# A sixteen-entry decoder on one core: the order of the last three entries, and half of the first entry's mixing products on VectorE

## The chip, the cores and the metric

One Trainium2 chip, one of its cores. The metric is the device time of one execution of the whole program in microseconds (us), less is better. TensorE is called PE in the views, VectorE DVE, ScalarE ACT, GpSimd POOL, and SP is the engine that issues all DMA transfers here.

## What is computed

Sixteen independent batch entries of 256 tokens by 256 features run through six layers, each followed by a layer norm. Cut to what matters:

```python
x = _layernorm(x + _L0_attn_ref(x, ...))      # q, k, v per token; kv and qkv mix the 16 heads of ONE token; then a gelu MLP
x = _layernorm(x + _L0_xattn_ref(x, ctx, ...))  # 16 heads, window of 64 to either side
x = _layernorm(x + _L0_ffn_ref(x, ...))       # a cell of 6 nodes, each an 8-head attention
x = _layernorm(x + _L1_attn_ref(x, ...))      # causal, linear, 16 heads
x = _layernorm(x + _L1_xattn_ref(x, ctx, mask, ...))  # 16 heads against the context
x = _layernorm(x + _L1_ffn_ref(x, ...))       # a product with a matrix made from a Fourier transform
```

In the first layer each token has its own small product over heads:

```python
kv = jnp.einsum('bhnd,bhne->bnde', k, v)
qkv = jnp.einsum('bhnd,bnde->bhne', q, kv)
```

The kernel computes it as q k for each pair of heads of a token, and then that times v. This is what is called mixing below.

## The kernel before

Four entries are in flight at a time (`NS = 4`), each in its own slots of SBUF. Entry i + 4 is loaded when entry i is finished. The work of an entry is a list of steps, made by `entry_steps`: each names its engine, an operation, a cost in us that is only a planning number, what it needs and which PSUM banks it takes and frees. `setup_steps` does the same for the work that is done once: products of weights (`fold`, `cb`, `four`, `nb`, `ob`, `n5`), for which TensorE multiplies and VectorE or ScalarE evicts, and `scale`, six pairs of scalings of weights on GpSimd (L1627, L1628).

`program_plan` plays these steps through with the planning costs and writes down, engine by engine, the order in which they came. That order is what every engine then executes: an engine never passes over a step that waits. Among the steps that are ready on an engine the planner takes the one of the lowest entry number first (the set-up counts as 1.5, on SP as 2.5), and among those the one with the longest chain of steps behind it (`tail`). The tails are multiplied by random factors drawn from the numbers in `SEEDS`, so that a different list of seeds gives a different order among steps of one entry. A tail is the same for all entries. The planner also chooses the PSUM banks (`pick`): a score product takes two pairs of banks, most others one.

The steps that the text speaks of:

- `mix1` and `mix2`: the mixing of an entry, in 16 pieces of two heads. For each piece GpSimd makes the products q k (L1641) and VectorE sums them (L1217), then GpSimd multiplies by v (L1651) and VectorE sums again (L1221). Pieces of one parity share a buffer. `mixn` divides (L1226, L1228, L1232), then `o_t` transposes the result on TensorE (L733), and the entry goes on with `a_o`, `fc`, `down`.
- Attention heads come as `s` (scores, L886), `nm` (the negated row maxima transposed, L896), `st` (scores transposed and the maxima added, L908 and L920), `pv` (L947), for the nodes of the cell also L954. VectorE takes the maxima (L1260) and splits them (L1266, L1269), ScalarE takes the exponentials (L1491). An entry has 4 groups in the second layer, 12 in the cell, and 4 in the fifth layer, the groups 16 to 19, called the y heads.
- `r_t` to `rpv`: the fourth layer. `y_t`, `y_q`, `y_o`, `f_t`, `f`: the last two. All products of a whole weight matrix are L740 or L748.
- `store` writes the entry's result (L1770).

The middle of the program is periodic: from one entry to the next TensorE gets the same 146 steps.

## Time and profile before

| | |
|---|---|
| median of 3 runs | 3439.23 us (3435.72 to 3452.06) |
| the profiled execution | 3441.86 us, its span 3440.1 us |
| PE busy | 3101.7 us, 90% of the span |
| DVE, ACT, POOL busy | 2330.8, 1701.0, 1182.5 us |
| mean granted clock of TensorE | 0.967 of full speed |

The span is from the first instruction of the program to the last; the time is 1.8 us longer. A busy TensorE is one with a matmul on it, at whichever clock. The granted clock is full (1.0, 2.4 GHz) or half (0.5, 1.2 GHz), and a number between these says how a stretch was shared.

### The profile page before, as it was taken

Reading aid. Unit: us, or ns where it says so; the run is one execution under the profiler, and the core shown is the slowest. Engines: PE = TensorE matmul, PEld = TensorE weight load, DVE = VectorE, ACT = ScalarE, POOL = GpSimd, SP = SyncE. Lnnn points to the kernel's source line nnn. Section 1 sums busy time; section 2 is a strip of 40 time slices with the busy share of each in tenths; the row PEclk is TensorE's granted clock in tenths of the full one; section 3 lists DMA queues with packets and bytes.
Section 4 is the critical chain, followed back from the end, with each engine's and each line's share of the span. In section 5 each row is a group of like instructions: output and inputs, shape, how many; then the busy total and the mean of one; then the engine's idle time right before and its main releaser. Section 6 shows DMA issues by size and latency. Waiting matters only on the chain.

```text
span 3440.1 us, 75934 instructions
## 1 busy us (share of the span) xinstructions
PE 3101.7 (90%) x29836; PEld 2294.8 (67%) x29836; DVE 2330.8 (68%) x5044; ACT 1701.0 (49%) x3496; POOL 1182.5 (34%) x1308
## 2 busy tenths in 40 slices
PE   7889889999999999989999999999999999989876
PEld 6766666676666666666666766666676666666654
DVE  6586667768686866768677686867767686465543
ACT  1245454555546455554545555464554545454442
POOL 7876007062341615234170623416052341100000
PEclk8899999999999999999999999999999999999996
DMA  7211001010101101011110101011010110100000
GB/s 223 72 56 35 20 29 35 26 47 20 43 27 38 29 26 47 20 39 32 35 32 25 49 20 43 27 38 29 22 52 20 39 32 20 32 14 10 10 10 4
DMA packets 123275, 122.77 MB, mean 36 GB/s; under 512 B 9776, under 2 KB 122672, under 8 KB 122800
## 3 DMA queue, kind: packets, MB, share of 16 engines
q1 hardware_dynamic: 122928, 117.91, 11.6%
q8 instruction: 246, 4.03, 0.5%
q14 instruction: 101, 0.83, 0.1%
HBM read 113.69 MB, written 4.19 MB: 34 GB/s over the span
## 4 chain that ended last, share of the span: by engine, by line
PE 63%; DVE 15%; ACT 7%; POOL 7%; issue 7%; DMA 1%; SPq 0%; DVEq 0%; POOLq 0%; ACTq 0%
PE banks L748 18%; PE banks L740 16%; PE banks L886 7%; DVE nmx L1260 6%; PE banks L947 5%; PE banks L908 5%; ACT work L1491 4%; POOL work L1641 3%; PE banks L733 2%; POOL work L1651 2%; PE banks L954 2%; PE banks L851 2%; POOL work L1661 1%; DVE added L1278 1%; ACT work L1393 1%
## 5 line engine op out<-in xcount | busy, mean ns | idle before, releaser
L748 PE MATMUL banks<-work,weights 128*128 128x256 f32 x3584 | 848.6, 385 | 22.5 <-DVE work L1284 10.4
L748 PEld LDWEIGHTS banks<-work,weights 128*128 128x128 f32 x3584 | 662.5, 190 | 153.6 <-issue 43.4
L1260 DVE TENSOR_REDUCE nmx<-banks 128x4 f32<-128x1024 f32 (+1 forms) x567 | 609.5, 1115 | 200.5 <-PE banks L886 199.0
L1491 ACT ACTIVATE work<-banks 128x1024 f32<-128x1024 f32 (+3 forms) x703 | 598.4, 908 | 270.5 <-PE banks L920 251.4
L740 PE MATMUL banks<-weights,work 128*128 128x256 f32 x2688 | 665.8, 395 | 20.2 <-DVE work L1288 7.6
L740 PEld LDWEIGHTS banks<-weights,work 128*128 128x128 f32 x2688 | 506.6, 195 | 131.9 <-issue 37.0
L1651 POOL TENSOR_TENSOR work<-work 128x512 f32<-128x512 f32 x256 | 417.6, 1655 | 85.1 <-DVE work L1221 81.9
L908 PE MATMUL banks<-work 32*128 32x256 f32 (+1 forms) x5120 | 367.1, 397 | 70.1 <-DVE nmx L1260 42.1
L886 PE MATMUL banks<-work 32*128 32x256 f32 (+1 forms) x5120 | 361.2, 398 | 70.5 <-DVE nmx L1260 29.7
L1641 POOL TENSOR_TENSOR work<-work 128x512 f32<-128x512 f32 x256 | 335.5, 1333 | 132.0 <-DVE work L1217 108.6
L1695 POOL TENSOR_TENSOR work<-work,row 128x512 f32<-128x512 f32 x64 | 93.0, 1463 | 836.8 <-PE banks L733 836.8
L1278 DVE TENSOR_TENSOR added<-work 128x1024 f32<-128x1024 f32 x192 | 264.4, 1378 | 150.3 <-ACT work L1491 111.1
L908 PEld LDWEIGHTS banks<-work 32*128 32x128 f32 x5120 | 235.8, 189 | 191.2 <-DVE nmx L1260 81.0
L947 PE MATMUL banks<-work 128*32 128x256 f32 (+3 forms) x5632 | 333.6, 358 | 31.3 <-DVE nmx L1260 15.6
L886 PEld LDWEIGHTS banks<-work 32*128 32x128 f32 x5120 | 238.9, 189 | 158.4 <-issue 102.3
L947 PEld LDWEIGHTS banks<-work 128*32 128x32 f32 x5632 | 157.0, 109 | 172.9 <-issue 96.5
L1393 ACT ACTIVATE work<-banks,cb 128x256 f32<-128x256 f32 x384 | 160.8, 470 | 202.8 <-PE banks L748 202.8
L1217 DVE TENSOR_REDUCE work<-work 128x32 f32<-128x512 f32 x256 | 172.5, 683 | 127.0 <-POOL work L1641 127.0
L1661 POOL TENSOR_SCALAR_AFFINE_SELECT work<-work 128x128 f32<-128x128 f32 (+1 forms) x512 | 161.2, 362 | 256.2 <-ACT work L1491 256.2
L1221 DVE TENSOR_REDUCE work<-work 128x32 f32<-128x512 f32 x256 | 173.0, 681 | 87.1 <-POOL work L1651 86.9
L1475 ACT ACTIVATE work<-banks 128x256 bf16<-128x256 f32 x320 | 116.7, 387 | 162.4 <-PE banks L896 162.2
L1254 DVE CUSTOM_DVE_ANT_0 banks<-banks,band 128x192 f32<-128x192 f32 x512 | 165.7, 393 | 27.5 <-PE banks L886 27.4
(160 smaller groups left out, 3540.7 us busy)
## 6 DMA issues: line engine op xcount, KB each, us to landing
weights<-in_w_all SPq DMA_DIRECT2D x322, 256.0 KB, 2.7
work<-in_w_setup SPq DMA_DIRECT2D x41, 256.0 KB, 5.0
work<-in_ctx SPq DMA_DIRECT2D x32, 256.0 KB, 3.0
work<-in_x SPq DMA_DIRECT2D x16, 256.0 KB, 3.0
out<-work SPq DMA_DIRECT2D x16, 256.0 KB, 2.2
weights<-in_w_all SPq DMA_DIRECT2D x1, 3072.0 KB, 15.6
row<-in_rows SPq DMA_DIRECT2D x1, 1280.0 KB, 9.0
mrow<-in_mask SPq DMA_DIRECT2D x16, 32.0 KB, 3.3
```

The source lines that it names most:

```text
L740: ins = e.matmul(b[:, m * 256:m * 256 + 256], xin[:, k, m * P:m * P + P], wslot(w)[:, k, :], start=(k == 0 and (m == 0 or closed)) if star ...
L748: ins = e.matmul(b[:, m * 256:m * 256 + 256], wslot(w)[:, k, m * P:m * P + P], xin[:, k, :], start=(k == 0 and (m == 0 or closed)) if star ...
L886: ins = e.matmul(b[g // 2][g % 2][:, cc * 256:cc * 256 + kk.stop - kk.start], q[32 * g:32 * g + 32, f, cc * P:cc * P + P], k[32 * g:32 * g ...
L908: e.matmul(b[g // 2][g % 2][:, o], k[32 * g:32 * g + 32, f, kc * P:kc * P + P], q[32 * g:32 * g + 32, f, qq], start=(kc == 0), stop=False, ...
L947: ins = e.matmul(b[32 * g:32 * g + 32, lo:hi], left, right[:, kc * 256 + lo - qq.start:kc * 256 + hi - qq.start], start=(kc == 0), stop=(k ...
L1260: ins = e.tensor_reduce(nmax(s, n)[:, 2 * p + j:2 * p + end, :], b.rearrange("p j (c n) -> p j c n", c=NC)[:, :, :, 0:w], AX, ALU.max, neg ...
L1278: e.tensor_tensor(added[:, half], pt(half, 0, 4)[:, :, 0:S], pt(half, 0, 4)[:, :, S:2 * S], ALU.add).then_inc(*tell(vec[s], "added", a, i))
L1393: ins = e.activation(dst[:, c, :], halves(src)[:, c, :], ACT.Identity, scale=w(c) if w else 1.0, bias=bias(c) if bias else 0.0)
L1491: ins = e.activation(dst, b.rearrange("p j (c n) -> p j c n", c=NC)[:, :, :, 0:w], ACT.Exp)
L1641: e.tensor_tensor(big1, q.unsqueeze(2).broadcast_to([P, PH, NH, DH]), k.unsqueeze(1).broadcast_to([P, PH, NH, DH]), ALU.mult).then_inc(*te ...
L1651: e.tensor_tensor(big2, mix.unsqueeze(2).broadcast_to([P, PH, DH, NH]), v.unsqueeze(1).broadcast_to([P, PH, DH, NH]), ALU.mult).then_inc(* ...
L1661: ins = e.affine_select(out=part, in_=part, compare_op=ALU.is_ge, fill=0.0, base=base, pattern=[[0, 2], [sign, hi - lo]], channel_multipli ...
```

## The change

Two rules of the planner change, and the list of seeds.

1. In the choice among ready steps the entry's number is replaced by `min(w[0], NB - 3)`. For entries 0 to 12 nothing changes; 13, 14 and 15 are equal, and among them the step with the longest chain behind it goes first.
2. For entry 0 the odd pieces' `mix1` and `mix2` products are put on VectorE. They become the operations `product1` and `product2`, with a planning cost of 0.65 us. These are 16 products, with the same operands as GpSimd's.
3. `SEEDS` loses one number in the middle and gets four new ones at the end.

```diff
-SEEDS = (519167, ..., 279811, 642892, 207843, ..., 237616)
+SEEDS = (519167, ..., 279811, 207843, ..., 237616, 902168, 809533, 586745, 617725)
...
+    def engine(i, n):
+
+        e, op, a = steps[n][:3]
+        return "DVE" if i == 0 and e == "POOL" and op in ("mix1", "mix2") and a % 2 else e
+
...
-                waiting[steps[n][0]].append((i, -tail[n], n))
+                waiting[engine(i, n)].append((i, -tail[n], n))
...
-                    ((2.5 if e == "SP" else 1.5) if w[0] < 0 else w[0]) + (0 if kept_mode(w[2]) else 0.5), w[1], w[2])):
+                    ((2.5 if e == "SP" else 1.5) if w[0] < 0 else min(w[0], NB - 3)) + (0 if kept_mode(w[2]) else 0.5), w[1], w[2])):
...
+                if steps[n][0] == "POOL" and e == "DVE":
+                    op, us = {"mix1": "product1", "mix2": "product2"}[op], 0.65
...
+                elif op == "product1":
+                    q, k, v, mix, big1, big2 = mix_views(s, a)
+                    if a < 2:
+                        e.wait_ge(*when("elu", 0, i))
+                        e.wait_ge(*when("elu", 1, i))
+                    else:
+                        e.wait_ge(*when("mix", a - 2, i))
+                    e.tensor_tensor(big1, q.unsqueeze(2).broadcast_to([P, PH, NH, DH]),
+                                    k.unsqueeze(1).broadcast_to([P, PH, NH, DH]), ALU.mult).then_inc(
+                        *tell(vec[s], "mix products", a, i))
+                elif op == "product2":
+                    q, k, v, mix, big1, big2 = mix_views(s, a)
+                    e.wait_ge(*when("mix", a, i))
+                    if a < 2:
+                        e.wait_ge(*when("a_qkv", 2, i))
+                    else:
+                        e.wait_ge(*when("mix sum", a - 2, i))
+                    e.tensor_tensor(big2, mix.unsqueeze(2).broadcast_to([P, PH, DH, NH]),
+                                    v.unsqueeze(1).broadcast_to([P, PH, DH, NH]), ALU.mult).then_inc(
+                        *tell(vec[s], "mix values", a, i))
```

The new lines shift the line numbers: what is L733, L740, L748, L886, L896, L908, L920, L947 before is L740, L747, L755, L893, L903, L915, L927, L954 in the changed kernel, and the VectorE lines L1207, L1212, L1217, L1221 are L1214, L1219, L1224, L1228. The new products are L1236 and L1246.

TensorE, the end of the program. Before, the last rows are the y heads of entry 15 and its `y_o`, `f_t`, `f`:

```order
L908 MATMUL banks<-work 128x256 x8
L920 MATMUL banks<-work,ones_bf 128x512 x4
L896 MATMUL banks<-ident_bf,nmx 128x128 x4
L947 MATMUL banks<-work 32x256 x8
L908 MATMUL banks<-work 128x256 x8
L920 MATMUL banks<-work,ones_bf 128x512 x4
L947 MATMUL banks<-work 32x256 x8
L908 MATMUL banks<-work 128x256 x8
L920 MATMUL banks<-work,ones_bf 128x512 x4
L947 MATMUL banks<-work 32x256 x16
L740 MATMUL banks<-weights,work 128x256 x4
L733 MATMUL banks<-ident,work 128x128 x4
```

In the changed kernel the same place holds the last `st` and `pv` of entries 14, 15 and 13, then `f` of 13, `y_o` of 14 and 15 in one row of 12, and `f_t` and `f` of 14 and of 15:

```order
L954 MATMUL banks<-work 32x256 x8
L915 MATMUL banks<-work 128x256 x8
L927 MATMUL banks<-work,ones_bf 128x512 x4
L954 MATMUL banks<-work 32x256 x8
L740 MATMUL banks<-ident,work 128x128 x4
L954 MATMUL banks<-work 32x256 x8
L747 MATMUL banks<-weights,work 128x256 x12
L740 MATMUL banks<-ident,work 128x128 x4
L747 MATMUL banks<-weights,work 128x256 x4
L740 MATMUL banks<-ident,work 128x128 x4
L747 MATMUL banks<-weights,work 128x256 x4
```

Three entries' ends now stand among each other. In the planner's lists, TensorE's last 62 of 2366 steps are entry 15's alone before; in the changed kernel entry 13 has its last step 7 from the end, and the last 104 steps hold all of `r_t` to `f` of the entries 13, 14 and 15. Entry 12 ends 335 steps (4326 matmul records) before the end in the one, 326 steps (4158 records) in the other.

VectorE, the first mixing. Before, after the bias additions (L1207) and the second half of the elu (L1212), there are only sums of the mixing (L1217, L1221) and evictions of set-up products (L1129, L1125):

```order
L1212 SCALAR_TENSOR_TENSOR work<-work 128x512 x2
L1207 TENSOR_TENSOR work<-banks,row 128x512
L1212 SCALAR_TENSOR_TENSOR work<-work 128x512
L1207 TENSOR_TENSOR work<-banks,row 128x512
L1217 TENSOR_REDUCE work<-work 128x32 x2
L1221 TENSOR_REDUCE work<-work 128x32
L1129 TENSOR_TENSOR cb<-banks,ews 128x3x2
L1221 TENSOR_REDUCE work<-work 128x32
L1217 TENSOR_REDUCE work<-work 128x32
L1207 TENSOR_TENSOR work<-banks,row 128x512
L1217 TENSOR_REDUCE work<-work 128x32
L1125 TENSOR_SCALAR weights<-banks,ews 128x512
```

In the changed kernel at the same place:

```order
L1219 SCALAR_TENSOR_TENSOR work<-work 128x512 x2
L1214 TENSOR_TENSOR work<-banks,row 128x512
L1236 TENSOR_TENSOR work<-work 128x512
L1219 SCALAR_TENSOR_TENSOR work<-work 128x512
L1224 TENSOR_REDUCE work<-work 128x32 x2
L1246 TENSOR_TENSOR work<-work 128x512
L1236 TENSOR_TENSOR work<-work 128x512
L1228 TENSOR_REDUCE work<-work 128x32
L1224 TENSOR_REDUCE work<-work 128x32
L1228 TENSOR_REDUCE work<-work 128x32
L1246 TENSOR_TENSOR work<-work 128x512
L1224 TENSOR_REDUCE work<-work 128x32
```

All 16 products (L1236, L1246) and nearly all sums of entry 0 stand ahead of the first eviction of a set-up product, which before was the seventh of these rows. On GpSimd three of the six scalings now stand between the even pieces' products of entry 0; before, the first came after them all.

TensorE, the y heads of one entry in the periodic middle. Before, two `st` (L908, L920) follow four `s`:

```order
L886 MATMUL banks<-work 128x256 x8
L896 MATMUL banks<-ident_bf,nmx 128x128 x2
L886 MATMUL banks<-work 128x256 x8
L908 MATMUL banks<-work 128x256 x8
L920 MATMUL banks<-work,ones_bf 128x512 x4
L908 MATMUL banks<-work 128x256 x8
L920 MATMUL banks<-work,ones_bf 128x512 x4
L896 MATMUL banks<-ident_bf,nmx 128x128 x4
L947 MATMUL banks<-work 32x256 x8
```

and in the changed kernel the first `st` comes after two `s`, and `s`, `pv` and `st` alternate:

```order
L893 MATMUL banks<-work 128x256 x8
L903 MATMUL banks<-ident_bf,nmx 128x128 x4
L755 MATMUL banks<-work,weights 128x256 x4
L915 MATMUL banks<-work 128x256 x8
L927 MATMUL banks<-work,ones_bf 128x512 x4
L893 MATMUL banks<-work 128x256 x8
L903 MATMUL banks<-ident_bf,nmx 128x128 x2
L954 MATMUL banks<-work 32x256 x8
L893 MATMUL banks<-work 128x256 x8
L915 MATMUL banks<-work 128x256 x8
L927 MATMUL banks<-work,ones_bf 128x512 x4
```

In the periodic middle some 20 of 146 TensorE steps stand in another order, all of them here, and one pair of cell products (`ck` and `eq`) changes places twice.

## Rows read from the trace of the kernel before

**Rows 1.** The page: span, and PE busy and granted clock in 40 slices

```profile
span 3440.1 us, 75934 instructions
...
PE   7889889999999999989999999999999999989876
...
PEclk8899999999999999999999999999999999999996
```

**Rows 2.** SP's timeline: the stores of entries 12 and 15 (start, duration)

```profile
2909.84 0.38 SPq L1770 DMA_DIRECT2D out<-work  x1
...
3437.52 0.38 SPq L1770 DMA_DIRECT2D out<-work  x1
```

**Rows 3.** Stretch, its us, busy PE, PEld, DVE, ACT, POOL (instructions), PEclk, DMA

```profile
2909.80:3106.00 196.20, 179.60 (x1850) 131.60 (x1846) 110.21 (x254) 103.89 (x212) 20.42 (x50) 0.98 0.07 22
3106.00:3296.00 190.00, 169.60 (x1689) 120.57 (x1689) 103.94 (x194) 93.02 (x189) 10.73 (x23) 0.95 0.04 11
3296.00:3440.00 144.00, 91.16 (x764) 63.86 (x762) 56.50 (x108) 44.26 (x92) 4.51 (x6) 0.77 0.02 6
```

**Rows 4.** The same for two periods of the middle

```profile
903.40:1101.70 198.30, 183.57 (x1840) 135.31 (x1841) 144.30 (x312) 105.88 (x219) 73.57 (x79) 1.00 0.11 33
...
1908.10:2107.50 199.40, 183.96 (x1841) 135.38 (x1840) 144.15 (x311) 106.09 (x219) 72.93 (x79) 1.00 0.12 33
```

**Rows 5.** PE by line and shape, 3296 to 3440: busy, mean ns, idle

```profile
L740 PE MATMUL banks<-weights,work 128*128 128x256 f32 x80 | 24.4, 462 | 7.9 <-DVE work L1288 2.8 <-ACT work L1418 2.3 <-DVE work L1284 1.5
L908 PE MATMUL banks<-work 32*128 32x256 f32 x128 | 13.6, 558 | 3.7 <-ACT work L1475 2.1 <-issue 1.4 <-ACT work L1491 0.2
```

**Rows 6.** The same for the period 1707 to 1908

```profile
L740 PE MATMUL banks<-weights,work 128*128 128x256 f32 x168 | 40.4, 386 | 0.3 <-DVE work L1284 0.2
...
L908 PE MATMUL banks<-work 32*128 32x256 f32 x256 | 18.2, 398 | 4.2 <-DVE nmx L1260 3.5 <-issue 0.7
```

**Rows 7.** PE's longest waits, 3296 to 3440: total, times, longest

```profile
PE banks L733 <- DVE work L1201: 12.5, 3, 6.7
PE banks L896 <- DVE nmx L1269: 10.4, 3, 4.1
```

**Rows 8.** Busy time by stretch: `r_t` to the end, and `y_o` to the end

```profile
3355.00:3440.00 85.00, 52.50 (x436) 36.79 (x436) 32.36 (x67) 24.76 (x53) 3.52 (x4) 0.70 0.01 4
3422.90:3440.00 17.10, 7.50 (x20) 4.92 (x20) 4.85 (x14) 1.59 (x5) 1.26 (x1) 0.63 0.05 15
```

**Rows 9.** GpSimd and VectorE by line during the first mixing, 27.8 to 86.6

```profile
L1651 POOL TENSOR_TENSOR work<-work 128x512 f32<-128x512 f32 x18 | 27.4, 1536 | 2.0 <-DVE work L1217 2.0
L1641 POOL TENSOR_TENSOR work<-work 128x512 f32<-128x512 f32 x18 | 23.5, 1318 | 2.2 <-DVE work L1217 2.2
...
L1217 DVE TENSOR_REDUCE work<-work 128x32 f32<-128x512 f32 x18 | 12.0, 680 | 3.7 <-POOL work L1641 3.7
```

**Rows 10.** Timelines of VectorE and GpSimd, 85 to 92

```profile
85.97 0.69 DVE L1232 TENSOR_TENSOR work<-work,head 128x512 f32<-128x512 f32 x1
...
86.74 1.27 POOL L1667 TENSOR_TENSOR work<-work,row 128x512 f32<-128x512 f32 x1 [3.01 <-DVE work L1232]
...
90.43 1.58 POOL L1627 TENSOR_SCALAR weights<-weights,ewb 128x512 f32<-128x512 f32 x1
```

**Rows 11.** Two VectorE lines in the whole run: duration ns min/median/max, first and last start

```profile
L1212 DVE SCALAR_TENSOR_TENSOR work<-work x32: 682/691/1929, 25.1 to 2729.5; 128x512 f32<-128x512 f32 x32
...
L1159 DVE TENSOR_TENSOR weights<-weights,wsum x2: 1695/1696/1697, 52.1 to 62.2; 128x512 f32<-128x512 f32 x2
```

**Rows 12.** PE's timeline: entry 0's `o_t`

```profile
86.87 0.60 PE L733 MATMUL banks<-ident,work 128*128 128x128 f32 x4
```

**Rows 13.** Busy time by stretch: the start, in two parts

```profile
14.10:86.90 72.80, 66.21 (x285) 57.42 (x286) 50.68 (x91) 9.00 (x18) 56.63 (x41) 0.79 0.69 220
86.90:152.10 65.20, 55.32 (x293) 46.63 (x291) 39.61 (x92) 16.24 (x33) 61.52 (x46) 0.94 0.31 90
```

**Rows 14.** Busy time by stretch: y heads of entry 7, from the third `s`

```profile
1862.50:1884.60 22.10, 17.16 (x254) 10.32 (x253) 14.13 (x31) 13.95 (x24) 0.00 (x0) 1.00 0.01 2
```

More of the change, by code:

```diff
@@ L71 @@
 RSLOT = {n: i for i, n in enumerate(ROWS)}
[L73 removed]
+SEEDS = (519167, 634534, 875864, 704644, 851259, 37516, 529412, 612800, 351972, 744357, 284174, 279811, 207843, 86077, 805968, 561942, 32633, 126238, 798516, 91813, 237616, 902168, 809533, 586745, 617725)
 SLOTS = 10
```

1 line of the change is left out of this document (removed).

## Prediction, made before the changed kernel ran

> **What bounds the kernel now.** I read the page first: TensorE is the busiest engine, and the 40 slices show it at eight or nine tenths everywhere but in the last three, where the granted clock falls in the last one too [rows 1]. Then the stretches between stores. In the periodic middle one entry costs 198.3 us, of which TensorE is busy 183.6, and the next sample reads 184.0 of 199.4; so the pace of the middle is 92.4% busy at a clock of 1.00 [rows 4]. VectorE has 144 us of work in the same time and GpSimd 73. The middle is bound by TensorE, and there only fewer gaps can help.
>
> The end is another thing. Entry 12's store is issued at 2909.8 and entry 15's at 3437.5 [rows 2], those of 13 and 14 at 3106 and 3296, and in the three stretches from store to store TensorE is busy 179.6 of 196.2 us, 169.6 of 190.0, and 91.2 of 144.0 us [rows 3]. In the last stretch entry 15 is alone. The reader is to see two losses in it: 53 us without a matmul, and a granted clock of 0.77, at which the same matmul takes longer: L740 462 ns in place of 386, L908 558 in place of 398 [rows 5, 6]. The idle time is that of one chain of steps with nothing beside it: TensorE waits for a layer norm's last step on VectorE (12.5 us in 3 waits) and for the split maxima (10.4 us) [rows 7].
>
> **The end, costed.** First the size of the pool. The two dearest lines of the last stretch would cost 24.4 x 386/462 = 20.4 and 13.6 x 398/558 = 9.7 us at full clock, 7.9 us less than they do [rows 5, 6]; I take 4.3 us more for the other 53 us of matmuls, so 79 of the 91.2 us remain. After entry 12's store there are then 179.6 + 169.6 + 79 = 428 us of TensorE work. At the pace of the middle (92.4%) that is 463 us; it takes 530.2 us now. So 67 us is the most that a perfect end gives back. By stretch: 2 us in the first, 6 in the second, 59 in the last. Three entries in flight are thus as good as four, two nearly, one is not.
>
> The change keeps three entries in flight until the last hundred steps, so nearly all of the lone stretch is gone. What is paid for it: the three entries reach the same layer together. From `r_t` to the end, entry 15 alone takes 85.0 us, with 32.4 us of VectorE and 52.5 us of TensorE at a clock of 0.70 [rows 8]. At full clock I estimate TensorE at 43 us of it: the last 144 us lose 12 of 91 us to the clock, 13%, and with 0.30 in place of 0.23 missing from the clock that becomes 18% of 52.5. Three times this is 129 us of TensorE and 97 us of VectorE. At the middle's pace it would be 140 us. VectorE has 0.75 of TensorE's work here and 0.78 in the middle [rows 4], so no engine takes TensorE's place as the bound; but the chain score, maxima, split, transposition, exponential, product is gone through by twelve groups of heads at the same time on 8 banks, with no long product of another layer to cover it. I take 20 us on top of the 140, half way between no loss (0) and 40 us. The very last steps, `y_o` to the end, are one chain in either kernel: 17.1 us with 7.5 busy [rows 8], of which two other entries can fill only the beginning; 10 us are lost. So 30 of the 67 us are paid again, and the end gains **37 us** (bounds: 67 - 10 = 57 us with no loss but the chain, and 67 - 10 - 40 = 17 us).
>
> Entry 12 itself ends 168 matmul records later; at 199 us for 1840 records [rows 4] its store comes 18 us later than before. This costs nothing, since the work that went ahead of it is no longer to do behind it.
>
> **The start, costed.** TensorE's first product waits 14 us for the first layer norm, which stays. Entry 0's `o_t` runs at 86.9 us [rows 12], 0.2 us after its mixing ends. In the mixing GpSimd makes 36 products in 50.9 us and waits 4.2 [rows 9]; 32 are entry 0's. GpSimd is the bound of entry 0 there. The change takes 16 products of 1.32 and 1.54 us away, 22.9 us, and puts three pairs of scalings in between that came behind (1.58 us each [rows 10], 9.5 us in all). It leaves a gain of 13.4 us if a product on VectorE costs what such an instruction costs alone, 0.69 us for 512 columns [rows 10].
>
> It does not. The instruction with that price, L1232, ran while GpSimd was idle for 3.01 us [rows 10]. L1159 is the same operation on 512 columns with both operands in SBUF, ran twice while GpSimd multiplied, and took 1.70 us both times; L1212, with two SBUF operands too, takes 691 ns in the median and up to 1929 [rows 11]. The sums, with one operand, show no such spread. So a VectorE product beside a stream of GpSimd products waits for the one under way, and the stream in turn waits for it. I price the 16 products at 1.4 us, nearer to L1159 than to the 0.69 of an idle GpSimd (bounds 0.69 and 1.93), with some 11 us of waiting on VectorE, and 16 x 0.69 = 11 us that GpSimd's stream is held up. That leaves 13.4 - 11 = 2.4 us of the gain.
>
> The Trainium skill says so in general ("SBUF — State Buffer", section "Who interferes with whom"): a VectorE instruction with two SBUF inputs and a GpSimd instruction that reads SBUF exclude each other for a whole instruction, and the later one blocks. The trace agrees, with 1.70 against 0.69 us. By a VectorE product at 0.69 us the start would gain 13 us; by this rule it gains next to nothing.
>
> What is queued behind matters as well: on VectorE nearly the whole mixing now stands ahead of the evictions of the set-up products. TensorE has only 8 banks; after nine set-up products and biases it must wait for the VectorE queue. Before, it worked through them with 6.6 us idle up to `o_t` [rows 13]. VectorE has 16 products at 1.4, 27 sums at 0.68 [rows 9] and some 3.5 us of other work from 25 us on, so it frees the bank that the fold of `v` of node 0 needs at about 69 us, where TensorE wants it at about 56 (that is when it made this product before). Some 10 us of idle come in there. They are partly paid back, since the postponed products then fill later gaps: 86.9 to 152.1 has 9.9 us idle [rows 13]. Sum for the start: -2.4 + 10 - 7, taken as **0 us** (bounds -12 and +15).
>
> **The middle, costed.** No operation is added. The y heads of each entry stand in another order: from the third `s` to the following layer TensorE is busy 17.2 of 22.1 us, 4.9 us idle [rows 14]. That is what a better order can win at most and, I assume, as much as a worse one would lose. In the new order the first exponential starts about a score product earlier, but the first `pv` then waits for it with one product in between where there were two. These nearly cancel; I take 0.4 us gained per entry, for the 13 entries that pass through it in this form: **-5 us** (bounds, at 1 us per entry to either side, -13 and +13).
>
> **Sum.** -37 + 0 - 5 = -42 us on the profiled execution's own 3441.9 us: 3399.9. That execution is 2.7 us over the median of the three runs, so against the median I predict **3397 us**, 1.2% less.
>
> **The rivals.**
> *The end keeps the middle's pace* (chance 0.14): TensorE and VectorE interlock without loss, as in the stretch 2909.8 to 3106, which has three entries in it and a clock of 0.98 [rows 3]. Against it: those three were in different layers. Then 57 us at the end, 5 in the middle: 3377 us.
> *VectorE holds up the start* (0.16): the products cost 1.9 us, the banks come free later still, and the 7 us are not paid back: +15 us. With the rest as forecast 3412 us.
> *The new order of the y heads is worse* (0.07): TensorE stands idle 3 us more per entry, in place of 0.4 less; over 13 entries 39 us, which cancels the gain: 3441 us. For it: TensorE's waits in this place are already for VectorE's maxima. Against: the operations and their number are the same.
> *The three ends do not overlap* (0.05), the case on the other side. If the twelve groups of y heads and the layer norms of the three entries form one chain through VectorE, `r_t` to the end takes three times 85.0 us = 255 us [rows 8], against the 170 us of my sum (140 + 20 + 10). That is 85 us more: 3482 us. It decides from about 212 us on, where the gain of 42 is used up. Against it: the stretch with two entries lost only 6 us.
>
> **How the numbers follow.** The forecast itself has a chance of 0.58. Its own range is 3378 to 3415 us. Less than 0.5%, 17 us, can't be told from no change here. Below 3422 lie the forecast, the first rival, and most of the second: faster 0.86. Between 3422 and 3456 lie the third and the unlucky sums of small losses: 0.09. Slower 0.05. For 8 times in 10 the range reaches from a bit under the first rival to a bit over the second: 3362 to 3428 us.
>
> **What the profile would show.** The stores of 13, 14 and 15 within about 15 us of each other at the end, and entry 12's some 18 us later than now. From entry 12's store to the end 465 to 485 us, in place of 530. The granted clock near 0.95 until some 20 us before the end. the last 104 TensorE steps in some 170 us. L1236 and L1246 with a mean near 1.4 us, and not 0.69. Entry 0's `o_t` at 80 to 87 us, with a wait of TensorE for VectorE's fold evictions ahead of it. The distance between middle stores within 1 us of 199.5. The forecast is wrong if the three last entries wait for each other's banks or VectorE by more than the 20 us that I gave them, or if the middle's period moves by more than 1 us, since that counts thirteen times.

## The result, and the profile after

The changed kernel takes 3425.77 us in the median, the kernel before 3449.28 us in the runs beside it; the ratio is 0.9941, 95% interval [0.9924, 0.9959], a gain of 20 us. The ratio and its interval leave out one execution of each kernel that took far longer (4289 and 9857 us). Forecast were 42 us and a range of 3378 to 3415 us. The direction is right and the size is not.

The profiled execution of the changed kernel takes 3425.71 us, 16 less than that of before. Its page (span; PE busy and granted clock in 40 slices):

```profile
span 3424.0 us, 75954 instructions
...
PE   6988999998998999999999999999989988999987
...
PEclk8899999999999999999999999999999989999999
```

Against [rows 1] the last three slices of PE read 987 where they were 876, and the clock does not fall at the end. In exchange there are new eights at the 33rd and 34th slice, and the clock falls in the 33rd, 2739 to 2825 us, ahead of entry 12's store. SyncE's timeline has the stores (start, duration):

```profile
2958.92 0.38 SPq L1797 DMA_DIRECT2D out<-work  x1
...
3409.35 12.36 SPq L1797 DMA_DIRECT2D out<-work  x3
```

The last three stores lie within 12.4 us of each other, but entry 12's comes 49 us later than in [rows 2]. The profiled change is then +49 up to that store and -65 behind it, in all -16. Busy time by stretch (stretch; us; busy PE, PEld, DVE, ACT, POOL; clock; DMA share; GB/s):

```profile
2733.90:2952.80 218.90, 187.42 (x1899) 137.85 (x1895) 151.86 (x411) 105.17 (x219) 92.84 (x137) 0.91 0.10 29
2952.80:3424.00 471.20, 421.90 (x4170) 298.25 (x4166) 266.34 (x477) 233.10 (x470) 13.83 (x19) 0.95 0.03 10
2958.90:3424.00 465.10, 416.65 (x4112) 294.74 (x4104) 260.45 (x465) 231.63 (x465) 13.51 (x18) 0.95 0.03 10
3280.80:3424.00 143.20, 116.86 (x1341) 82.77 (x1340) 104.74 (x231) 75.74 (x170) 11.53 (x14) 0.95 0.07 22
```

From entry 12's store to the end it takes 465 us instead of 530, at a clock of 0.95; the last row is the last 104 steps. That part of the forecast held. The first row does not fit it: 146 steps, a period's number, take 219 us, and TensorE is idle for 31 of them. In the middle a period has 15 us of idle time [rows 4].

For all later comparisons I place the steps of TensorE's order in the trace by counting matmul records. Step 1747 is the last mark at which the kernels are still in the middle, at step 1893 entry 12 is at its third node, step 2039 is where entry 12 has just ended.

| us | start to step 1747 | 1747 to 1893 | 1893 to 2039 | 2039 to end of TensorE |
|---|---|---|---|---|
| before | 2511.8 | 201.5 | 204.4 | 516.7 |
| changed | 2519.9 | 214.0 | 218.9 | 465.4 |

The end gives 51 us. The 292 steps ahead of it take 27 us more, and the start and middle 8. The 8 are no cost of the edits: ten of the runs below have, with the changed kernel's order of TensorE from step 287 to step 1747, 2003 to 2036 us in it, where the changed kernel has 2014 and before 2006. The 12 to 15 us of the stretch 1747 to 1893 are more than such a spread: the orders without the early levelling take 198.5 to 204.3 us there, and the changed kernel and the two runs with its order there (E6, E18) 214.0 to 215.1.

### The profile page after: what moved, and what is told of

Same layout as the page of the kernel before. It is cut to its first block, busy times and chain, and to the rows that moved or that the text cites. A ratio compares the mean times of both kernels' runs of the same rounds, so it can differ in the third digit from the quotient of the medians.

```text
span 3424.0 us, 75954 instructions
## 1 busy us (share of the span) xinstructions
PE 3101.5 (91%) x29836; PEld 2290.3 (67%) x29836; DVE 2353.5 (69%) x5040; ACT 1701.8 (50%) x3495; POOL 1167.6 (34%) x1292
## 4 chain that ended last, share of the span: by engine, by line
PE 61%; DVE 14%; POOL 10%; issue 7%; ACT 7%; DMA 1%; SPq 0%; DVEq 0%; POOLq 0%; ACTq 0%
PE banks L755 18%; PE banks L747 14%; PE banks L893 7%; PE banks L954 6%; PE banks L915 6%; DVE nmx L1287 5%; POOL work L1668 5%; ACT work L1518 3%; POOL work L1688 3%; PE banks L740 2%; POOL work L1678 2%; PE banks L858 2%; PE banks L961 2%; PE banks L927 1%; DVE added L1305 1%
## 5 line engine op out<-in xcount | busy, mean ns | idle before, releaser
L755 PE MATMUL banks<-work,weights 128*128 128x256 f32 x3584 | 857.8, 388 | 15.1 <-ACT work L1518 6.5
L755 PEld LDWEIGHTS banks<-work,weights 128*128 128x128 f32 x3584 | 668.4, 192 | 151.0 <-issue 48.7
L747 PE MATMUL banks<-weights,work 128*128 128x256 f32 x2688 | 658.6, 392 | 14.7 <-DVE work L1311 5.2
L747 PEld LDWEIGHTS banks<-weights,work 128*128 128x128 f32 x2688 | 501.3, 193 | 124.8 <-issue 41.0
L893 PE MATMUL banks<-work 32*128 32x256 f32 (+1 forms) x5120 | 363.5, 399 | 83.6 <-DVE nmx L1287 31.7
L1678 POOL TENSOR_TENSOR work<-work 128x512 f32<-128x512 f32 x248 | 406.9, 1663 | 85.1 <-DVE work L1228 83.2
L915 PE MATMUL banks<-work 32*128 32x256 f32 (+1 forms) x5120 | 371.3, 400 | 60.6 <-DVE nmx L1287 36.4
L1668 POOL TENSOR_TENSOR work<-work 128x512 f32<-128x512 f32 x248 | 330.3, 1354 | 133.4 <-DVE work L1224 110.3
L954 PE MATMUL banks<-work 128*32 128x256 f32 (+3 forms) x5632 | 336.8, 361 | 34.5 <-POOL work L1688 24.8
L915 PEld LDWEIGHTS banks<-work 32*128 32x128 f32 x5120 | 237.9, 190 | 175.2 <-issue 101.4
L893 PEld LDWEIGHTS banks<-work 32*128 32x128 f32 x5120 | 240.0, 189 | 171.4 <-issue 114.8
L954 PEld LDWEIGHTS banks<-work 128*32 128x32 f32 x5632 | 158.3, 110 | 178.4 <-issue 120.7
L1224 DVE TENSOR_REDUCE work<-work 128x32 f32<-128x512 f32 x256 | 171.8, 682 | 107.1 <-POOL work L1668 107.0
L1688 POOL TENSOR_SCALAR_AFFINE_SELECT work<-work 128x128 f32<-128x128 f32 (+1 forms) x512 | 161.6, 362 | 241.0 <-ACT work L1518 241.0
L1228 DVE TENSOR_REDUCE work<-work 128x32 f32<-128x512 f32 x256 | 172.8, 680 | 83.2 <-POOL work L1678 83.0
L1281 DVE CUSTOM_DVE_ANT_0 banks<-banks,band 128x192 f32<-128x192 f32 x512 | 165.4, 391 | 34.7 <-PE banks L893 34.4
```

Of the source, the lines that this page charges most:

```text
L747: ins = e.matmul(b[:, m * 256:m * 256 + 256], xin[:, k, m * P:m * P + P], wslot(w)[:, k, :], start=(k == 0 and (m == 0 or closed)) if star ...
L755: ins = e.matmul(b[:, m * 256:m * 256 + 256], wslot(w)[:, k, m * P:m * P + P], xin[:, k, :], start=(k == 0 and (m == 0 or closed)) if star ...
L893: ins = e.matmul(b[g // 2][g % 2][:, cc * 256:cc * 256 + kk.stop - kk.start], q[32 * g:32 * g + 32, f, cc * P:cc * P + P], k[32 * g:32 * g ...
L915: e.matmul(b[g // 2][g % 2][:, o], k[32 * g:32 * g + 32, f, kc * P:kc * P + P], q[32 * g:32 * g + 32, f, qq], start=(kc == 0), stop=False, ...
L954: ins = e.matmul(b[32 * g:32 * g + 32, lo:hi], left, right[:, kc * 256 + lo - qq.start:kc * 256 + hi - qq.start], start=(kc == 0), stop=(k ...
L1228: e.tensor_reduce(q, big2, AX, ALU.add).then_inc(*tell(vec[s], "mix sum", a, i))
```

## Experiments

All ratios are to the kernel before, timed beside it on the same chip. The lines of a kernel with the late rule (E7, E9, E10, E11, E15, E16) are one higher than those of the changed kernel.

### Which of the three edits is it? (E1 to E4)

The edits are: the numbers (`SEEDS`), the products (`engine`), the rule (`min(w[0], NB - 3)`). Each kernel is the changed one with some of them undone:

```diff
 E1  -SEEDS = (... of the change)   +SEEDS = (... of before)
 E1  -        return "DVE" if i == 0 and ... else e   +        return e
 E2  -SEEDS = (... of the change)   +SEEDS = (... of before)
 E2  -... min(w[0], NB - 3)   +... w[0]
 E3  -        return "DVE" if i == 0 and ... else e   +        return e
 E3  -... min(w[0], NB - 3)   +... w[0]
 E4  -... min(w[0], NB - 3)   +... w[0]
```

E1, the rule only. 

> Only the rule for the last three entries, with the numbers and the mixing of before. Theory A (the rule itself pushes entry 12 back: with entries 13 to 15 equal, the work of 14 and 15 that fills entry 12's gaps is other work than before, and the x layer's selects queue behind their mixing on GpSimd): entry 12's store comes 25 to 45 us later than in before (2935 to 2955 us), the stretch after it is some 65 us shorter, and the whole is 15 to 25 us faster. Theory B (the new numbers cost the time, the rule gives the full gain that was forecast): entry 12's store comes some 5 us from before's and the whole is 35 to 50 us faster. Theory C (the products on VectorE cost it): as B.

E2, the products only. 

> Only the first entry's odd products on VectorE, with the numbers and the priorities of before. Theory A: within 5 us of before. Theory B: within 5 us. Theory C: 10 to 25 us slower, with the first entry's o_t steps later than 86.9 us or the middle's periods longer than 199 us.

E3, the numbers only. 

> Only the new list of numbers. Theory A: within 5 us of before, periods of the middle within 1 us of 199. Theory B: 10 to 25 us slower, of it some 8 us in the middle (that much later step 1747 of TensorE's order) and the rest after it. Theory C: within 5 us of before.

E4, numbers and products without the rule. 

> The changed kernel without the rule for the last three entries (new numbers, and products on VectorE). Theory A: within 5 us of before, with entry 12's store at 2905 to 2920 us. Theory B and C: 15 to 30 us slower than before, since the loss is there and the gain of the end is not; entry 12's store at 2930 to 2945 us.

| | ratio | 95% interval |
|---|---|---|
| E1 rule only | 0.9998 | 0.9976 to 1.0021 |
| E2 products only | 1.0478 | 1.0452 to 1.0505 |
| E3 numbers only | 1.0394 | 1.0366 to 1.0421 |
| E4 numbers and products | 0.9996 | 0.9976 to 1.0017 |

E4 says that numbers and products together are worth nothing (1 us, within 8), so on the new numbers the gain is the rule's: 0.9941 / 0.9996 = 0.9945, 19 us, known to some 9 us. In E1 the rule gains nothing at all on the old numbers: from step 1747 to 2039 it takes 451 us (before 406), from there 463 (before 517). Theory A thus named the right two stretches, and the loss ahead is still larger than it had said; entry 12's store comes at 2962.6 us, later than its 2935 to 2955. No theory had expected the figures of E2 and E3. Neither edit touches an instruction of the middle, and yet every period of the middle (steps 287 to 1747) takes 202 to 228 us in place of 198 to 205. The changes are not additive: each edit alone costs 135 to 165 us, of which 124 to 127 in the middle, and both together cost nothing.

### Do the products cost that, or the order? (E5, E6)

E5 takes the plan of before as it is and moves the 16 products from one engine's list to the other's after planning; E6 moves them back in the plan of the changed kernel.

```diff
+    taken = [(t, (i, names[op], a, u)) for t, (i, op, a, u) in timed["POOL"] if i == 0 and op in names and a % 2]
+    plan["POOL"] = [s for _, s in timed["POOL"] if not (s[0] == 0 and s[1] in names and s[2] % 2)]
+    plan["DVE"] = [s for _, s in sorted(timed["DVE"] + taken, key=lambda v: v[0])]
```

E5. 

> The kernel before, with the order of every engine as it was, but the first entry's 16 odd products taken out of GpSimd's order and put into VectorE's at the places of their planned times. E2 moved them and let the planner lay out everything anew, and took 165 us more. Theory A (it is the order that the planner makes from the changed starting times, above all in the middle, that cost the 165 us): within 12 us of before. Theory B (the products themselves hold up VectorE and, through it, the rest): 100 us and more slower.

E6. 

> The changed kernel with its order on every engine, but the 16 products put back on GpSimd at the places of their planned times. Theory A (the move is worth nothing by itself, as its o_t came 4.6 us earlier and step 287 at the same time): within 5 us of the changed kernel, that is a ratio to before of 0.989 to 0.998. Theory B (GpSimd's longer chain, 11 us more by the durations of rows 9 and 11, decides the start): 8 to 12 us slower than the changed kernel, ratio 0.996 to 1.000.

E5: 1.0022 [0.9997, 1.0047], E6: 0.9950 [0.9928, 0.9972] (the changed kernel had 0.9941 in its own comparison). E5 thus costs 8 us (-1 to +16) and not 165: the 165 us of E2 are the order that the planner laid out anew around the products. Theory A held there. E6 does not decide between its theories. Its ratio is 3 us from the changed kernel's, but the interval reaches into theory B's 0.996 to 1.000, and its one profiled execution, the slowest of its twelve, shows theory B's size at the start: `o_t` at 93.6 us and step 287 at 518.5, against 82.3 and 505.9 with the products on VectorE. The nine other runs with the changed kernel's start reach step 287 at 500.8 to 506.6. So within the new order the products on VectorE give some 12 us up to there by that one profile, and what is left of it at the end isn't known.

### Does the order cost because it never repeats? (E13, E14)

In before and in the changed kernel the planned order of a period's 146 steps takes only three forms over the middle, in E2 it is another one in every period, in E3 one comes back only after four. Adding one number to the old list gives orders of either kind:

```diff
 E13 -..., 237616)   +..., 237616, 3)
 E14 -..., 237616)   +..., 237616, 6)
```

E13. 

> The kernel before with one number (3) added at the end of its list. Its planned order of TensorE's steps differs from entry to entry up to step 1163 and from there to step 2039 is the same 146 steps for each entry. Theory A (an order that does not repeat costs, whatever edit made it): periods of 207 to 220 us up to step 1163 and of 198 to 206 us behind it; ratio 1.010 to 1.030. Theory B (the harm of E2 and E3 lies in their own edits): within 10 us of before.

E14. 

> The kernel before with one number (6) added at the end of its list; its planned order is another one for each of the twelve periods. Theory A: periods of 207 to 222 us all along, ratio 1.035 to 1.055 as in E2 and E3. Theory B: within 10 us of before.

E13: 1.0465 [1.0436, 1.0493]. E14: 1.0455 [1.0427, 1.0483]. Two periods of E13 in its repeating half:

```profile
2000.20:2218.70 218.50, 194.32 (x1844) 140.73 (x1840) 142.70 (x313) 105.96 (x220) 72.02 (x79) 0.95 0.10 29
2218.70:2433.80 215.10, 191.44 (x1845) 139.25 (x1841) 142.91 (x313) 105.80 (x220) 71.91 (x79) 0.96 0.11 32
```

My theory fell on its own prediction: E13's repeating periods take 214 to 220 us, longer than several of its irregular ones (205 to 209). What both runs do show is that one more random number, and nothing else, makes this kernel 4.6% slower. E14's ratio lies where theory A had it, but after E13 this doesn't speak for the theory. The work is the same: 143 us of VectorE, 106 of ScalarE and 72 of GpSimd, as in [rows 4]. TensorE is idle 24 us per period instead of 15, and its clock is 0.95 to 0.96 instead of 1.00, and the same 1840 or so matmuls take 8 to 11 us longer. Which property of an order does it stays open. TensorE's waits in E13 (line waited at, engine and line waited for; us, times, longest), 1226 to 2400 us:

```profile
PE banks L908 <- DVE nmx L1260: 16.4, 18, 1.4
PE banks L886 <- DVE nmx L1260: 12.9, 12, 1.7
PE banks L886 <- ACT work L1393: 10.6, 8, 1.9
PE banks L896 <- DVE nmx L1260: 8.5, 15, 0.7
```

They are many short ones for the row maxima, none of them a new kind.

### Does it matter when the entries are made level? (E7, E9 to E11, E15, E16)

```diff
+        late = any(j == NB - 4 and o == "rpv" for j, o, _, _ in plan["PE"])
         for e in waiting:
...
-... min(w[0], NB - 3)
+... (min(w[0], NB - 3) if late else w[0])
```

That is E7; it takes effect from the first of entry 12's two `rpv` steps on, TensorE's step 1975. E10 has `"f"` for `"rpv"`, E11 `"co"` of node 2. E9 and E15 are E7 and E10 with the numbers and the mixing of before. E16 is E10 with four entries (`NB - 4`, and `NB - 5` in `late`).

E7. 

> The changed kernel, with the last three entries put level only once entry 12's last step of the attention to the kept rows has been issued on TensorE. Theory A (while entry 12 runs, the levelled entries 14 and 15 fill its gaps with work that collides, 29 us of time ahead of step 2039 against E4; the drain's gain needs only the levelling behind it): entry 12's store at 2915 to 2930 us, the stretch behind it 475 to 495 us, whole 3395 to 3415 us, ratio 0.984 to 0.990. Theory B (the loss is what the drain's gain is bought with: the work of 14 and 15 done early is what is missing late): the stretch behind entry 12's store is 495 us or more and the whole within 8 us of the changed kernel.

E10. 

> As E7, but level only once entry 12's last product (the step f, TensorE's step 2030) is issued, some 52 steps later than in E7. Theory A (only work ahead of entry 12's store that the levelling pulls forward costs anything): steps 1747 to 2039 take 403 to 408 us, as without the rule, entry 12's store comes at 2915 to 2930 us, and the drain behind it still ends the three entries together, 480 to 495 us behind it; ratio within 0.003 of E7's. Theory B (what a levelling costs ahead it must pay back behind, one for one): the stretch behind entry 12's store is longer by what is saved ahead of it, and the same ratio as E7 comes out too, but with entry 12's store more than 10 us earlier and the drain more than 10 us longer.

E11. 

> As E7, but level already from entry 12's third node on (TensorE's step 1888), some 90 steps earlier than in E7 and 140 later than the changed kernel's levelling begins to show. Theory A (cost grows with how long entry 12 shares TensorE with levelled entries): entry 12's store 10 to 25 us later than in E7, ratio between E7's 0.984 and the changed kernel's 0.994. Theory B (only the first levelled steps, 1747 to 1893, cost something): within 0.002 of E7's ratio.

E9. 

> The kernel before (its numbers, its mixing) with the rule of E7, level once entry 12's attention to the kept rows is issued. Theory A (the late levelling is worth about 50 us by itself; numbers and products only decide which repeated order the middle falls into, and both repeated orders take the same time): ratio 0.981 to 0.989, with periods of the middle of 198 to 206 us. Theory B (the new list of numbers and the products are needed for the gain): ratio 0.992 to 1.000.

E15. 

> The kernel before (its numbers, its mixing) with the rule of E10: the last three entries level once entry 12's last product is issued. If the gain is the drain's alone: steps 1747 to 2039 take 403 to 410 us, step 2039 to the end 455 to 465 us instead of 517, ratio 0.982 to 0.988. If the numbers and the products have a part in it: ratio 0.989 to 0.996.

E16. 

> The changed kernel, with the last four entries level once entry 11's last product is issued. If a drain is better the more entries end together: step 1893 to the end is 10 us and more shorter than E10's. If the levelled entries wait for one another at the same kinds of step (the loss ahead in the changed kernel): steps 1893 to 2185 take 20 to 40 us more than E10's, and what the end gains over E10 is under 15 us; ratio 0.988 to 0.996.

| | level from | ratio | 95% interval | 1747 to 2039, us | idle in it | 2039 to end, us |
|---|---|---|---|---|---|---|
| changed | start | 0.9941 | 0.9924 to 0.9959 | 432.9 | 48.8 | 465.4 |
| E11 | step 1888 | 0.9869 | 0.9836 to 0.9903 | 425.8 | 46.3 | 462.2 |
| E7 | step 1975 | 0.9838 | 0.9800 to 0.9876 | 416.3 | 39.6 | 462.6 |
| E10 | step 2030 | 0.9848 | 0.9815 to 0.9880 | 404.0 | 29.1 | 457.0 |
| E4 | never | 0.9996 | 0.9976 to 1.0017 | 403.5 | 31.2 | 524.1 |
| E9 | as E7 | 0.9890 | 0.9862 to 0.9919 | 414.7 | 41.0 | 462.7 |
| E15 | as E10 | 0.9828 | 0.9800 to 0.9856 | 410.9 | 30.9 | 449.9 |
| E16 | step 1884, four entries | 0.9935 | 0.9910 to 0.9959 | 451.8 | 66.1 | 446.4 |

The columns of us are of one profiled execution each, and executions of one order differ: before, E5 and E15, whose TensorE order is the same up to step 2030, take 406, 409 and 411 us from 1747 to 2039. The sooner the levelling begins, the more is lost ahead of step 2039. By the intervals of their ratios E7, E10 and E11 are clear of the changed kernel; E11 and E7 are not told apart, and with entry 12's store at 2985.7 us, 55 after E7's, E11 missed theory A's 10 to 25. The drain behind it takes 457 to 465 us in the first four whenever it begins: what is done ahead buys nothing behind (against theory B of E7 and E10). The stretches 1893 to 2039 and 2039 to the end of E10:

```profile
2737.50:2943.00 205.50, 191.17 (x1848) 142.05 (x1849) 141.75 (x303) 109.46 (x224) 73.76 (x79) 0.99 0.12 35
2943.00:3405.70 462.70, 406.24 (x4213) 293.32 (x4211) 267.60 (x556) 232.12 (x477) 33.33 (x71) 0.96 0.04 13
```

Between E7 and E10 the profiles differ by 18 us behind step 1747 and the ratios by nothing that can be told. E15 has the lowest ratio, though its interval overlaps those of E7 and E10: the kernel before with nothing but the levelling of its last three entries from entry 12's last product on, 3393.54 against 3453.55 us, 1.7% less. New numbers and products were not needed. Its stretches were expected at 403 to 410 and 455 to 465 us; the second was shorter. E9's 0.9890 stands at the edge of what theory A gave it. E7's and E10's stores came at 2931.0 and 2930.2 us, and E10's drain takes 476 us from there, a little less than expected. E16 loses 40 us against E10 from step 1893 to 2185 and wins 15 back: four level entries lose more ahead than they win at the end.

### Which queue makes the loss ahead? (E8, E12)

```diff
 E8  +... min(w[0], NB - 3) if e != "POOL" else w[0]
 E12 +... min(w[0], NB - 3) if e == "PE" else w[0]
```

E8. 

> The changed kernel with the rule on all engines but GpSimd, where the entries keep their order. Theory A (the x layer's selects behind the mixing of entries 14 and 15 on GpSimd are the loss ahead of step 2039): TensorE's waits of line 954 on GpSimd halve there, step 2039 starts 10 to 20 us earlier than at 2952.8 us, whole 8 to 20 us faster than the changed kernel. Theory B (VectorE's row maxima and the order on TensorE are the loss): within 5 us of the changed kernel.

E12. 

> The changed kernel with its rule on TensorE's queue alone; VectorE, ScalarE and GpSimd keep the entries' order. Theory A (the loss ahead of step 2039 is made on TensorE's own order: steps of entries 14 and 15 stand between entry 12's and 13's): steps 1747 to 2039 still take 425 to 440 us, ratio 0.990 to 0.997. Theory B (it is made on VectorE and ScalarE, where maxima and exponentials of the levelled entries stand ahead of those that TensorE needs next): steps 1747 to 2039 take 403 to 415 us, ratio 0.984 to 0.990.

E8: 0.9921 [0.9897, 0.9946]; steps 1747 to 2039 take 448 us, step 2039 starts at 2952.4 us, and TensorE's waits at L954 for GpSimd's L1688 there are 5.1 us in 5, in place of 6.1 in 6. Theory A failed on all of these. E12: 0.9938 [0.9915, 0.9960], 443 us, 3 more than theory A's range, and far from theory B's. The rule on GpSimd's queue is thus not needed for the loss, and the rule on TensorE's alone is enough to make it. The planner lays out the other queues anew around TensorE's, so this doesn't say which engine TensorE then waits for.

### Which steps' levelling makes it? (E17, E18)

The two periods ahead of step 2039 are to be looked at one by one. From step 1747 to 1893, first the changed kernel, then E4:

```profile
2519.90:2733.90 214.00, 196.71 (x1840) 147.11 (x1840) 140.94 (x275) 111.08 (x229) 72.24 (x74) 0.98 0.14 41
2529.80:2728.40 198.60, 183.74 (x1840) 135.39 (x1840) 144.30 (x312) 105.78 (x219) 73.84 (x79) 1.00 0.11 33
```

TensorE is idle only 2 us more, and busy 13 us more with as many matmuls. They are other matmuls: with entry 14 level there are 14 steps of the first layer in this period in place of 11. The line of the step `down`, changed kernel, then E4:

```profile
L858 PE MATMUL banks<-weights,work 128*128 128x256 f32 x64 | 16.5, 416 | 0.1
L858 PE MATMUL banks<-weights,work 128*128 128x256 f32 x32 | 7.4, 385 | 0.1
```

Priced by the mean busy time of each kind of step in the middle, an estimate from the traces of before and E4, the 146 steps are 196 us of work in place of 186. So most of what is late at step 1893 is work done early, and can't be from x heads: there are 24 selects in it where there were 32.

In the second period the changed kernel's steps are lighter, by the same estimate 172 us of work in place of 186, and take 14 us more. Here is the time lost. TensorE's waits in it, 2733.9 to 2952.8 us:

```profile
PE banks L954 <- POOL work L1688: 3.3, 3, 1.4
PE banks L893 <- DVE nmx L1287: 3.2, 2, 1.7
PE banks L903 <- DVE nmx L1296: 2.7, 3, 1.8
PE banks L893 <- DVE nmx L1281: 2.4, 1, 2.4
...
PE banks L915 <- DVE nmx L1281: 2.1, 2, 1.4
```

L1281 and L1688 belong to the x layer (the attention with a band mask) alone. Their waits are 7.8 of 31 us of idle time, against 1.6 of 16 in E4. Both by line in that stretch, changed kernel, GpSimd and VectorE (instructions, busy us, mean ns, idle before):

```profile
L1688 POOL TENSOR_SCALAR_AFFINE_SELECT work<-work 128x128 f32<-128x128 f32 (+1 forms) x88 | 28.0, 361 | 56.2 <-ACT work L1518 56.2
L1281 DVE CUSTOM_DVE_ANT_0 banks<-banks,band 128x192 f32<-128x192 f32 x80 | 25.8, 390 | 2.4 <-PE banks L893 2.4
```

and in the same steps of E4:

```profile
L1688 POOL TENSOR_SCALAR_AFFINE_SELECT work<-work 128x128 f32<-128x128 f32 (+1 forms) x32 | 10.1, 367 | 12.5 <-ACT work L1518 12.5
L1281 DVE CUSTOM_DVE_ANT_0 banks<-banks,band 128x192 f32<-128x192 f32 x32 | 10.4, 392 | 1.6 <-PE banks L893 1.6
```

An entry has 32 of each. With the entries level the x layers of 13, 14 and 15 fall together: in TensorE's order there are 10 of the x layer's score steps in this stretch where there were 4. The same period in the other runs (selects counted by their time, one profile each):

| 1893 to 2039 | E4, E10, E17 | E7 | E9 | E11 | E16 | changed, E18 | E1 | E12 | E8 |
|---|---|---|---|---|---|---|---|---|---|
| selects | 32 | 56 | 61 | 64 | 80 | 88 | 88 | 88 | 88 |
| us | 201.8 to 205.5 | 214.7 | 213.2 | 218.2 | 240.7 | 218.9, 219.1 | 219.4 | 224.2 | 227.6 |
| TensorE idle, us | 14.3 to 16.4 | 24.9 | 24.5 | 30.0 | 49.8 | 31.5, 30.9 | 37.5 | 35.6 | 40.0 |

The idle time goes with the crowding, but isn't given by it. E17 and E18 split the rule by the kind of step, without any late beginning:

```diff
 E17 +... min(w[0], NB - 3) if w[2] > place["PE", "x_o", 0] else w[0]
 E18 +... min(w[0], NB - 3) if w[2] <= place["PE", "x_o", 0] else w[0]
```

E17. 

> The changed kernel, its rule only for the steps behind the x layer (behind x_o in the list of an entry); the steps up to there keep the entries' order. The x layers of 13, 14 and 15 are then not drawn together. Theory A (crowded x layers are the loss): 4 groups of x heads, 32 selects, in the stretch from step 1893 to 2039, which takes 203 to 210 us as in E4, and the drain from 2039 on still takes under 475 us; ratio 0.982 to 0.989. Theory B (any levelling beside entry 12 costs, whatever the kind of step): that stretch takes 214 us and more, ratio 0.990 to 0.997.

E18. 

> The complement of E17: the rule only for the steps up to x_o, the rest in the entries' order. Theory A: 10 groups of x heads fall in the stretch from step 1893 to 2039, which takes 215 to 222 us as in the changed kernel; the drain is in part as before, since the ends are level no more; ratio 0.996 to 1.006. Theory B: that stretch takes under 210 us, ratio 0.990 to 1.000.

E17: 0.9927 [0.9902, 0.9953]. E18: 1.0055 [1.0030, 1.0080]. Stretches 1893 to 2039 and 2039 to the end, first E17, then E18:

```profile
2727.10:2928.90 201.80, 186.99 (x1840) 137.52 (x1841) 141.30 (x303) 105.21 (x217) 73.74 (x79) 0.98 0.11 30
2928.90:3428.00 499.10, 421.79 (x4220) 302.64 (x4220) 266.91 (x551) 236.48 (x480) 33.48 (x71) 0.94 0.05 14
```

```profile
2732.90:2952.00 219.10, 188.20 (x1924) 137.85 (x1921) 153.21 (x417) 105.89 (x219) 92.27 (x136) 0.90 0.10 29
2952.00:3473.60 521.60, 441.05 (x4141) 311.06 (x4140) 264.42 (x469) 231.67 (x466) 15.51 (x19) 0.90 0.03 9
```

From step 1747 to 2039 E17 takes 403.2 us with 32 selects in the second period, and E18 433.1 us with 88, the loss of the changed kernel (432.9). This shows less than it was meant to. The plans of the kernels, laid side by side, say that E17's order of TensorE is E4's up to step 2066, and E18's that of the changed kernel up to step 2023: there is no levelled step behind the x layer in these two periods that could have cost anything. So the loss is made by the levelled steps of the first layer and the x layer, the only ones that are moved there, but theory B, that any levelling beside entry 12 costs, was not put to the test, nor were the x heads parted from the first layer's steps. E17's ratio lies in theory B's range. Its drain takes 493 us from step 2039 to TensorE's end, not under 475; entry 15 has its last 28 steps alone. E18 pays the loss and gains nothing at the end, which makes it slower than before.

So it is shown that the early levelling of these steps makes the loss, and where. That the crowded x layers are the reason is supported by the table and by the waits, and not shown: 6 of the 15 us more of idle time in the second period are waits for the x layer's own lines. Against it as the only cause stands E1, which is idle 30 us in the first period too, with 24 selects. Of the 29 us in all (432.9 less E4's 403.5) 17 are idle time of TensorE and 12 busy time. The latter is no larger amount of work: by the estimate above the two periods hold 368 us of it in place of 372. The clock of 0.94 in place of 0.99 goes with it.

## Why the prediction was off

**The end.** "After entry 12's store there are then ... 428 us of TensorE work", of which 465 to 485 us to the end were forecast: 465.1 was measured, and the ends within 15 us: 12.4. By the sum's own terms this stretch is 530 - 37 - 18 = 475 us, and by the rival that the end keeps the middle's pace 530 - 57 - 18 = 455; what was measured lies half way between. The terms within it were off both ways: the last 104 steps took 143 us where I had 170, so the 20 us for the entries in lockstep and most of the 10 for the last chain were not needed there, and the steps ahead of them took 322 us where 475 - 170 = 305 were left. In E10 and E15 the drain takes 457 and 450 us from step 2039, which is 60 to 67 us less than before's 517, so nearly the whole 67 us of the ceiling are to be had.

**Entry 12's store.** This is the step that failed: "its store comes 18 us later than before. This costs nothing, since the work that went ahead of it is no longer to do behind it." It came 49 us later. Eight of them are there before step 1747, and are the spread of single executions. 18 were counted. The other 23 are in none of its terms: what the sum put at nothing was the pace of the work ahead of the store. I had counted the records that the rule moves and priced them at the middle's pace, without looking at which kinds of step they are and come together with. Counting records was wrong both ways: from step 1747 to 1893 there are no more of them and 10 us more work, and from 1893 to 2039 there are 54 more and 14 us less work, by the estimate above, and that stretch is idle 31 us in place of 16. The levelled steps of the first layer and the x layer make it; what it is about them stays open, with the crowding of the x layers as the best supported reason. The order of the changed kernel could have raised the question beforehand: 10 x score steps in 146, where there were 4. The whole account on the profiled executions is then 42 forecast, 13 less from the middle (+8 for -5), 23 less from the store, 10 more from behind it (465 for 475): 16.

**The start, 0 us (bounds -12 and +15).** Held. `o_t` at 82.3 us was in the range of 80 to 87, and TensorE waits for the fold eviction as said, 8.0 us at most. The changed kernel's timeline and its longest waits up to 150 us:

```profile
82.28 0.85 PE L740 MATMUL banks<-ident,work 128*128 128x128 f32 x4
```

```profile
PE banks L740 <- DVE work L1208: 14.1, 1, 14.1
PE banks L765 <- DVE work L1214: 9.4, 2, 8.0
```

Step 287 comes at 505.9 us, before at 505.5. That the sum is nothing says little of its terms: moving the products alone costs 8 us (-1 to +16) in the order of before (E5), and taking them back in the new order costs 3 us in the ratio and 13 in one profile up to step 287 (E6), where the sum had 2.4 us of gain for them. The price of 1.4 us for a product was too high; VectorE by line, 20 to 90 us:

```profile
L1236 DVE TENSOR_TENSOR work<-work 128x512 f32<-128x512 f32 x8 | 8.6, 1077 | 0.0
L1246 DVE TENSOR_TENSOR work<-work 128x512 f32<-128x512 f32 x8 | 8.3, 1035 | 0.0
```

That is 1.06 us, and the two forms come to it in different ways (below).

**The middle, -5 us (bounds -13 and +13).** The profiles have +8 between steps 287 and 1747. The many executions decide: E4 has everything but the rule and stands at 0.9996, within 8 us. So it is 0, inside the bounds. The share of it that I had from the y heads can't be told from nothing. But the bounds were lucky. In E2, E3, E13 and E14 another list of numbers, or the products, makes the middle 124 to 140 us longer, ten times my bound, and nothing in the trace of before says so.

**The rivals.** The end came half way to the middle's pace; the three ends did overlap; VectorE didn't hold up the start as a whole; of the order of the y heads nothing can be told, since the middle didn't change. That the rule would cost time ahead of entry 12's store, in an earlier layer, was in none.

## What to carry to other kernels

When a priority is relaxed to let the last pieces of work end together, relax it only when the piece before them has ended: that gave 1.7% here, and the same rule from the start 0.0 to 0.6%. Steps moved forward are not priced by their number; price them by kind, count in the new order which kinds stand together, and ask what one unit of the bound engine's time then asks of the others. And where a planner lays everything out anew, try an edit also with the order frozen, since here the order alone could cost up to eight times the measured gain.

## What the runs showed of the hardware

A VectorE product of 512 columns beside GpSimd's stream (by duration, min/median/max ns):

```profile
L1236 DVE TENSOR_TENSOR work<-work x8: 673/738/1986, 27.4 to 56.5; 128x512 f32<-128x512 f32 x8
```

```profile
L1246 DVE TENSOR_TENSOR work<-work x8: 1008/1016/1183, 31.1 to 64.9; 128x512 f32<-128x512 f32 x8
```

Half of the first kind took no more than some 0.74 us, in the stretch in which GpSimd was multiplying, and the second never less than 1.01 us. The two differ only in how the operands are laid out and spread over the 512 columns: the first reads both operands in order, the second reads `v` at every sixteenth element (`mix_views`). Whether that costs the 0.3 us wasn't tried. GpSimd had its share of the waiting: in the same stretch its products take

```profile
L1678 POOL TENSOR_TENSOR work<-work 128x512 f32<-128x512 f32 x10 | 17.7, 1778 | 1.8 <-DVE work L1224 1.8
L1668 POOL TENSOR_TENSOR work<-work 128x512 f32<-128x512 f32 x11 | 17.1, 1559 | 2.3 <-DVE work L1224 2.3
```

against 1536 and 1318 ns in [rows 9], 0.24 us more each. The Trainium skill ("SBUF — State Buffer", section "Who interferes with whom") has the later of the two instructions blocked for the whole of the other. The maxima agree with that (1986 ns is about 673 and one GpSimd product of 1318); the median of 738 says that on most occasions VectorE came first or lost little, and the price is split between both engines.

TensorE's granted clock goes with its idle time in the period from step 1893 to 2039: 0.90 and 0.91 with 31 us idle of 219 (E18, changed), 0.87 with 50 of 241 (E16), 0.98 and 0.99 where it is idle 14 to 16 us (E4, E10, E17).
